# Rows 0 and 1: rotary keys copied out of PSUM by ScalarE and turned on GpSimd, with a new instruction order

## The reference

```python
_, idx = jax.lax.top_k(I, kk)                  # 96 keys for each query
key_c = (c_kv @ W_uk)[bi, idx]
kr_sel = (x @ W_kr)[bi, idx]                   # picked rotary keys
angles_k = jnp.arange(kk)[:, None] * theta[None, :] + delta    # by rank in the list
key_r = _pope(kr_sel, angles_k[None, None, :, :])
scores = (einsum(q_c, k_c) + einsum(q_r, key_r)) * scale
```

## Time and profile before

| | |
|---|---|
| median of 3 runs | 1168.19 us (1167.93 to 1173.78) |
| profiled execution, its own time | 1168.04 us |
| its span | 1166.3 us |
| busy: PE, DVE, ACT, POOL | 822.1, 890.1, 599.5, 299.4 us |
| granted TensorE clock, mean | 0.841 of full |

### The profile page before, as it was taken

The page is one execution under the profiler, slowest core; times in us unless marked ns, Lnnn a source line. Parts: engine busy times, 40 slices in busy tenths (PEclk is TensorE's granted clock), DMA queues, the critical chain, the costliest instruction groups (busy, mean ns, idle before and its releaser), DMA issues.

```text
span 1166.3 us, 29414 instructions
## 1 busy us (share of the span) xinstructions
PE 822.1 (70%) x11808; PEld 509.2 (44%) x11808; DVE 890.1 (76%) x2076; ACT 599.5 (51%) x1311; POOL 299.4 (26%) x224
## 2 busy tenths in 40 slices
PE   5666868888758885587674877467677774667784
...
DMA packets 85079, 72.20 MB, mean 62 GB/s; under 512 B 24784, under 2 KB 63696, under 8 KB 84752
## 3 DMA queue, kind: packets, MB, share of 16 engines
...
## 4 chain that ended last, share of the span: by engine, by line
DVE 30%; PE 24%; issue 18%; ACT 13%; POOL 8%; DMA 4%; SPq 2%; DVEq 0%; POOLq 0%; ACTq 0%
POOL big L1512 4%; PE bank L660 4%; DVE Y L2045 3%; DVE bank L1955 3%; PE bank L882 3%; PE bank L847 2%; ACT relu_s L1178 2%; DVE onehot L1735 2%; DVE relu_s L1623 2%; DMA big<-comb_rows 1%; DVE SG L1955 1%; POOL XP L1519 1%; SPq L593 1%; ACT QBD L1217 1%; PE bank L1006 1%
## 5 line engine op out<-in xcount | busy, mean ns | idle before, releaser
L1512 POOL TENSOR_TENSOR big<-DU,BC 128x1024 f32<-128x1024 f32 x64 | 150.5, 2358 | 168.0 <-DVE DU L1938 121.8
L1396 ACT ACTIVATE bank<-DEL,Aneg 128x512 f32<-128x512 f32 x128 | 87.8, 690 | 118.3 <-DVE CV L1962 42.1
L847 PE MATMUL bank<-onehot,tparts 128*32 128x256 bf16 x3840 | 124.8, 283 | 25.0 <-DVE onehot L1735 17.9
L847 PEld LDWEIGHTS bank<-onehot,tparts 128*32 128x32 bf16 x3840 | 101.1, 100 | 52.6 <-issue 30.6
L1006 PE MATMUL bank<-XP,CO 128*128 128x512 f32 x128 | 77.1, 720 | 31.2 <-POOL XP L1519 25.4
L1955 DVE TENSOR_TENSOR_SCAN bank<-bank,big 128x512 f32<-128x512 f32 x72 | 87.7, 1218 | 7.7 <-POOL big L1512 7.3
L1006 PE MATMUL bank<-CV,CO 128*128 128x512 f32 x128 | 74.8, 696 | 25.9 <-POOL CV L1519 23.0
L1451 POOL TENSOR_TENSOR fac<-em,den 128x16 f32<-128x16 f32 x16 | 5.0, 315 | 311.5 <-DVE den L1603 311.5
L1735 DVE TENSOR_SCALAR onehot<-ib,CO 128x1024 bf16<-128x1024 f16 x160 | 80.7, 548 | 2.6 <-PE bank L847 1.8
L1178 ACT ACTIVATE relu_s<-bank,nml 128x192 f32<-128x192 f32 (+1 forms) x128 | 52.8, 425 | 44.2 <-DVE nml L1691 43.9
L882 PE MATMUL bank<-GT,QBD 128*32 128x32 f32 x3072 | 54.5, 201 | 23.5 <-issue 15.3
...
## 6 DMA issues: line engine op xcount, KB each, us to landing
BC<-bc_rows SPq DMA_DIRECT2D x128, 256.0 KB, 4.4
...
rows_bounce<-RO SPq DMA_DIRECT2D x256, 8.5 KB
...
```

The lines of the kernel that those rows point to most:

```text
L847: m = mm(own.bank[3 - c % 2][32 * bb:32 * bb + 32, 256 * kind:256 * kind + 256], own.tparts[:, kt, part, 32 * kind:32 * kind + 32], onehot ...
L1396: A(own.bank[STATE_BANKS[j]][:, :], own.DEL[:, j, :], ACT.Exp, scale=Aneg[:, j, n:n + 1]).then_inc(dA_ok.sem, dA_ok.up(b))
L1512: pool.tensor_tensor(own.dBu[:, n % 2, :, :], own.DU[:, :, :], own.BC[:, n % ROWS_AHEAD, 0:1, :].to_broadcast([P, 2, L]), ALU.mult).then_i ...
```

## The change

For rows 0 and 1 (`turned_by_gpsimd`), DVE's multiplication L1744 goes: 32 instructions, four for each of eight tiles. In its place ACT copies the rotary half of the bank to SBUF (alternately into `SRd` and `PR`, which are free at that time) ahead of its latent copy, and POOL multiplies that copy by `rank_turn` into `GT[:, 1:3]`, with a new signal `gk_ok`. PE waits for `gk_ok` of all four chunks ahead of the picked scores; ACT waits for it ahead of chunks 2 and 3, whose copies go into a buffer used before. Some signals are merged to make room for the new one (the counting signals `hold_*` share one semaphore; gates and routing share signals), with the same waits. Rows 2 and 3 are as before. `ORDER` is new for all five engines over the whole program.

```diff
+        def turned_by_gpsimd(b):
+
+            return b < 2
...
                     pe.wait_ge(gt_ok.sem, gt_ok.at(b, 4 * i + 4))
+                    if turned_by_gpsimd(b):
+                        pe.wait_ge(gk_ok.sem, gk_ok.at(b, 4 * i + 4))
                     pe.wait_ge(g_sb.sem, g_sb.at(b, 4 * i + 4))
...
+                        if turned_by_gpsimd(b):
+                            if c >= 2:
+                                act.wait_ge(gk_ok.sem, gk_ok.at(b, 4 * i + c - 1))
+                            elif i >= 1:
+                                act.wait_ge(psum_ok.sem, psum_ok.at(b, i))
+                            A((own.SRd, own.PR)[c % 2][:, :, :].rearrange("p x j -> p (x j)"), own.bank[3 - c % 2][:, 256:512], ACT.Copy)
                         A(GT[:, 0, 8 * c:8 * c + 8, :].rearrange("p t j -> p (t j)"), own.bank[3 - c % 2][:, 0:256], ACT.Copy).then_inc(g_sb.sem, g_sb.up(b))
...
+                    if turned_by_gpsimd(b):
+                        for c in range(4):
+                            yield PART
+                            pool.wait_ge(g_sb.sem, g_sb.at(b, 4 * i + c + 1))
+                            PT(GT[:, 1:3, 8 * c:8 * c + 8, :], (own.SRd, own.PR)[c % 2][:, :, :].unsqueeze(1).to_broadcast([P, 2, 8, 32]),
+                               rank_turn[:, :, :].unsqueeze(2).to_broadcast([P, 2, 8, 32]), ALU.mult).then_inc(gk_ok.sem, gk_ok.up(b))
...
-                        TT(GT[:, 1:3, 8 * c:8 * c + 8, :], picked[:, 1:2, :, :].to_broadcast([P, 2, 8, 32]),
-                           rank_turn[:, :, :].unsqueeze(2).to_broadcast([P, 2, 8, 32]), ALU.mult)
+                        if not turned_by_gpsimd(b):
+                            TT(GT[:, 1:3, 8 * c:8 * c + 8, :], picked[:, 1:2, :, :].to_broadcast([P, 2, 8, 32]),
+                               rank_turn[:, :, :].unsqueeze(2).to_broadcast([P, 2, 8, 32]), ALU.mult)
                         dve.transpose(own.G[:, 8 * c:8 * c + 8, :], picked[:, 0, :, :]).then_inc(gt_ok.sem, gt_ok.up(b))
...
 ORDER = {
     "sync": (
-        7, 7, 11, 11, 16, 16, 16, 16, 16, 16, 32, 6, 1, 3, 15, 25, 16, 7, 5, 1, 11, 10, 1, 17, 36, 4, 11, 25,
+        0, 7, 18, 11, 16, 16, 16, 16, 16, 16, 32, 9, 2, 1, 3, 5, 1, 19, 26, 7, 11, 1, 5, 11, 1, 16, 31, 4, 5,
```

More of the change, by code:

```diff
@@ L330, in build @@
         s_setp = semaphore("setup_tensor")
-        hold_dve, hold_pe = semaphore("hold_vector"), semaphore("hold_tensor")
+        hold_dve = hold_pe = semaphore("hold_vector_or_tensor")
         hold_pool = hold_sp = semaphore("hold_gpsimd_or_sync")
@@ L365, in build @@
         gt_ok = signal("picked_keys_ready")
+        gk_ok = signal("picked_keys_turned_by_gpsimd")
         sr_ps = signal("picked_scores_in_psum")
@@ L400, in build @@
         rl_ps = signal("router_logits_in_psum")
-        rl_e = signal("router_exp_ready")
+        rl_e = signal("routing_exp_ready")
         comb_ok = signal("comb_ready")
-        ct_ps = signal("comb_t_in_psum")
-        ct_sb = signal("comb_t_in_sbuf")
+        ct_ps = signal("comb_then_gates_t_in_psum")
+        ct_sb = signal("comb_then_gates_t_in_sbuf")
         ga_ps = signal("gate_in_psum")
@@ L438, in build @@
         pm_ok = signal("gate_shifted")
-        pe_ok = signal("gate_exp_ready")
         mk_ok = signal("choice_ready")
@@ L443, in build @@
         cum_ok = signal("slots_taken_by_rows_ready")
-        gT_ps = signal("gates_t_in_psum")
-        gT_sb = signal("gates_t_in_sbuf")
         bias_ps = signal("bias_in_psum")
@@ L1054, in rest @@
                     m = turn(own.bank[2][0:NE2, i * P:(i + 1) * P], own.gate[:, i, :])
-                m.then_inc(gT_ps.sem, gT_ps.up(b))
+                m.then_inc(ct_ps.sem, ct_ps.up(b))
                 yield
-                pe.wait_ge(gT_sb.sem, gT_sb.at(b, 1))
+                pe.wait_ge(ct_sb.sem, ct_sb.at(b, 2))
                 pe.sem_inc(hold_pe, 1)
@@ L1408, in rest @@
                 act.wait_ge(pm_ok.sem, pm_ok.at(b, 1))
-                A(own.pr[:, 1, :, :], own.pr[:, 0, :, :], ACT.Exp).then_inc(pe_ok.sem, pe_ok.up(b))
+                A(own.pr[:, 1, :, :], own.pr[:, 0, :, :], ACT.Exp).then_inc(rl_e.sem, rl_e.up(b))
                 yield
                 yield
-                act.wait_ge(gT_ps.sem, gT_ps.at(b, 1))
-                A(own.GTs[:, :], own.bank[2][0:NE2, :], ACT.Copy).then_inc(gT_sb.sem, gT_sb.up(b))
+                act.wait_ge(ct_ps.sem, ct_ps.at(b, 2))
+                A(own.GTs[:, :], own.bank[2][0:NE2, :], ACT.Copy).then_inc(ct_sb.sem, ct_sb.up(b))
                 yield
@@ L1989, in rest @@
                 yield
-                dve.wait_ge(pe_ok.sem, pe_ok.at(b, 1))
+                dve.wait_ge(rl_e.sem, rl_e.at(b, 2))
                 dve.tensor_reduce(own.ps1[:, 1, :], own.pr[:, 1, :, :], AX.X, ALU.add).then_inc(vec.sem, vec.up(b))
@@ L2134 @@
     "sync": (
-        7, 7, 11, 11, 16, 16, 16, 16, 16, 16, 32, 6, 1, 3, 15, 25, 16, 7, 5, 1, 11, 10, 1, 17, 36, 4, 11, 25,
-        16, 7, 5, 1, 11, 11, 1, 16, 33, 29, 9, 1, 1, 6, 4, 1, 1, 1, 2, 2, 1, 1, 17, 23, 2, 2),
+        0, 7, 18, 11, 16, 16, 16, 16, 16, 16, 32, 9, 2, 1, 3, 5, 1, 19, 26, 7, 11, 1, 5, 11, 1, 16, 31, 4, 5,
+        1, 2, 19, 9, 5, 16, 7, 16, 7, 1, 2, 2, 1, 3, 1, 3, 17, 25, 29, 17, 1, 1, 1, 1, 2, 6, 3, 10, 28, 2, 2),
     "tensor": (
[10 rows of a table removed]
-    "scalar": (
[12 rows of a table removed]
[9 rows of a table added]
+    "scalar": (
[12 rows of a table added]
     "gpsimd": (
-        1, 1, 20, 20, 15, 15, 15, 15, 21, 15, 8, 7, 32, 12, 15, 20, 1, 3, 20, 22, 2, 1, 6, 20, 32, 12, 15, 20,
-        1, 3, 14, 38, 17, 5, 18, 28, 11, 1, 3, 2, 1, 2, 1, 1, 3, 2, 2, 2, 1, 1, 1, 2, 1, 1, 1, 1, 2, 2, 1, 2,
-        14, 23),
+        0, 1, 7, 6, 18, 18, 1, 1, 18, 18, 2, 1, 17, 3, 1, 15, 4, 1, 28, 25, 32, 28, 15, 3, 21, 30, 7, 1, 1,
+        16, 32, 12, 3, 2, 12, 15, 15, 21, 2, 3, 5, 20, 14, 5, 14, 8, 1, 2, 3, 1, 2, 2, 2, 15, 17, 1, 2, 1, 2,
+        3, 13, 37),
     "vector": (
[11 rows of a table removed]
[11 rows of a table added]
 }
```

## The result

The changed kernel takes 1191.01 us (median of 4 runs, 1182.32 to 1192.98) against 1168.06 us for the kernel before on the same chip (4 runs, 1165.50 to 1173.78): ratio 1.0177, interval 1.0131 to 1.0223. The ratios in this document are those on record, which compare only runs within 1.5% of the fastest of their kernel; they aren't quotients of the medians and differ from these by up to 0.4 points (the quotient here is 1.0196). The forecast was 1161.1 with a range up to 1175, so it missed in sign. The profiled execution took 1190.45 us, its span 1188.7.

What follows compares the result with a forecast made beforehand. From 60 to 330 us no engine is full, so freeing DVE alone can't shorten it one for one. 1168.0 - 1.9 (first stretch) + 0 (middle) - 5 (end) = 1161.1 us; range 1150 to 1175.

Steps and rivals of the forecast that it cites:

- What bounds the kernel: Attention of rows 0 and 1, 60 to 330 us: no engine full, DVE no more loaded than PE, GpSimd has room.
- Removed: First stretch: 32 DVE multiplications go, 21.9 us of DVE, of which 4.0 us lie on the chain: -4.0.
- ACT: Rows 0 and 1: 32 added copies of 0.37 us, 11.9 us of ACT, hidden inside a tile; waits cost nothing.
- POOL's own time: Rows 0 and 1: 32 multiplications at 1.28 us each, 41 us of POOL, bounded by 1.27 and 1.46.
- Last chunk: End of each tile: PE's scores wait for POOL, +0.5 us a tile; +2.0 for four cases, +4 for all eight.
- POOL against DVE: First stretch: POOL's work slows DVE by 0.11 us a microsecond, some 5 us for 41 us of POOL.
- 16 one-hots at +0.144 make +2.3: First stretch's chain: each of 16 one-hots slowed by 0.144 us beside POOL's work, +2.3 us.
- the forecast's band of 0.50 to 0.60: Before 345 us: expected mean one-hot time in us if the forecast holds; over 0.8 would show the third rival.
- The third rival: First stretch: POOL's turn and the next one-hot meet each time; +13.4, with the end's -5 1176.4 us; chance 0.18.
- Half of the costs covered by the new order: First stretch: other row's work hides half of 4.3 us of costs, giving -1.9 instead of +0.3.
- Middle, 0 within 4: Later attention, 345 to 850 us: no changed instructions, only another interleaving; 0, with 4 us either way.
- End, -5: Program's end: four groups of row 2's sums go ahead of row 3's last scan step; -5, bounds 0 and -7.4.

Runs made afterwards that it cites:

- e4: The kernel before plus ScalarE's 32 copies of the rotary half that nobody reads; ratio 1.0011 over the kernel before.
- c2: e2 plus ScalarE's 32 idle copies of the rotary half; ratio 1.0076 over the kernel before.
- e2: Old code (VectorE multiplies, no GpSimd turns) in the changed kernel's new order; ratio 1.0035 over the kernel before.
- f1: f0 plus the idle GpSimd multiplications of d1; 1176.59 us, ratio 1.0037 over the kernel before.
- f0: d4 again in more rounds; 1166.79 us against 1172.13 for the kernel before, ratio 0.9944.
- d1: e2 plus 32 idle GpSimd multiplications, started by each latent copy, that only a later DMA waits for; ratio 1.0183 over the kernel before.
- e6: Changed kernel with the old order up to a point in row 1's last tile, new order behind; ratio 1.0045 over the kernel before.
- d4: Old code (VectorE multiplies) with the orders of e6; ratio 0.9956 over the kernel before.
- b0: The kernel before, unchanged, run again on another chip for a profile; 1175.9 us beside a median of 1172.77.
- d2: d1 with each tile's four idle multiplications started together behind its last transpose; ratio 1.0184 over the kernel before.

## Why the prediction was wrong

**What bounds the kernel** was read right (no engine full), and the wrong thing was drawn from it: room on GpSimd is not free where GpSimd's work stops VectorE.

**Removed** (-4.0) and **ACT** (nothing): 32 multiplications went, as said, and ScalarE's copies cost 0.1 (e4) to 0.4 points (c2, against e2), not to be told from nothing; the forecast for ACT stands. That the 32 multiplications gave 4.0 us back on the chain is not borne out: idle work that frees nothing costs no more than the turns that free 21.9 us of VectorE (0.87 beside 0.95 points, 1.49 beside 1.35 to 1.42).

**POOL's own time**: 1.28 forecast, 1.32 measured. Right.

**Last chunk** (+2.0, 4 to 8 waits charged to GpSimd): one wait of 2.2 us was charged to it, and those for the transpose fell from 4.3 to 3.4. Together 5.6 instead of 4.3: right in size, and small.

**POOL against DVE** is the step that failed, "By that rate 41 us of POOL cost DVE some 5 us", and with it the term "16 one-hots at +0.144 make +2.3". VectorE was held 24.0 us, 0.57 a microsecond of turn and not 0.11, and GpSimd's load alone, idle, cost 10 to 17 us of the program's time (f1 against f0, d1 against e2). The rate came from three groups in a stretch where 155 us of GpSimd work lay beside all kinds of VectorE work, and the sum then charged one-hots alone. But here GpSimd doesn't start at random: the latent copy that starts the turn also starts VectorE's transpose, and what stands behind the transpose meets the turn. With the multiplication gone, nothing covers it, as I read it: idle work beside VectorE's multiplication holds VectorE 11.4 us (f1 against f0, one-hots 560 ns), the turn in its place 23.8 (e6 against d4, one-hots 12.0 of it). The mean of the one-hots, 564, fell into the forecast's band of 0.50 to 0.60, which I had taken for its confirmation; over two thirds of the held time lay on other instructions. The mean was a bad witness: of the 84 one-hots up to 366 us eight took 1.15 us or more, in b0 none.

The chain from 60 to 330 us, here in the changed kernel and below it in e2, shows how much of this became time:

```profile
by line: issue 19.3%; PE bank L849 10.2%; PE bank L662 6.1%; PE bank L886 6.0%; DVE onehot L1751 5.2%; DVE relu_s L1639 4.1%; ACT QBD L1221 4.0%; DVE top L1669 2.3%; PE bank L745 2.2%; DVE score L1674 1.9%; DVE ml L1702 1.9%; ACT PBD L1255 
...
by line: issue 18.7%; PE bank L849 8.4%; PE bank L886 6.3%; PE bank L662 5.7%; DVE onehot L1753 3.8%; ACT QBD L1221 3.4%; ACT PBD L1255 3.0%; DVE ml L1704 2.7%; DVE score L1658 2.7%; DVE G L1765 2.6%; DVE top L1671 2.4%; PE bank L745 2.3%; 
```

One-hots have 14.0 us of it and not 7.8, 10.3 in e2; `relu_s` L1639 has 11.1, where neither L1623 before nor its counterpart in e2 is among the rows shown. The share called issue, time in which the engine waited for nothing that the profile shows, went from 14.5% to 19.3%, 13 us more, and nearly all of that is in e2 too, where GpSimd turns nothing: it came with the new order. Why holds of this sum cost some 16 us in the new start and 4 to 11 in the old one stays open.

**The third rival** had the mechanism and a chance of 0.18. Its price, +13.4 for the first stretch, is near the 11 to 17 us that the turns cost (0.95 to 1.42 points); but that is in part luck: it charged all 32 turns, and eight one-hots were held for about a turn, with one-hots 6.2 us longer on the chain and not 13.4. Its sign of over 0.8 us for the mean one-hot was wrong for the same reason. Its place was too narrow as well: d2 shows that the load costs as much when one-hots don't meet it. "A mean of 0.144 also with POOL beside them" was the argument against it, and it was an average over places.

**Half of the costs covered by the new order** (-1.9 for the stretch) failed in sign. The new start costs 0.85 points by itself (e2 against d4 and f0), some 10 us. In e2's trace one-hots wait 7.0 us for TensorE's picks (9.9 and 4.9 in the two profiles of the changed kernel), which they didn't in the old order (0.2). That the moved positions of the one-hots are the cause is only argued: no run exchanges VectorE's list alone.

**Middle, 0 within 4**: it moved -5.4 and +13.6. The forecast said itself that over 4 us would make it wrong. All kernels of the table with the new rest show the second (276 to 283 us beside row 3's attention instead of 268), whatever their code, and the first against b0's 288.2 (279 to 283). It is the order; which part of it is open.

**End, -5** (bounds 0 and -7.4): -6.4 in the changed kernel, -5.2 to -6.6 in the others of the table with the new rest. Right, with its working: 41.9 us from the last scan step where under 45 was said.

The sum, corrected: +17.8 where -1.9 stood, 2.8 ahead of it that belongs to no step, +8.2 where 0 stood, -6.4 where -5 stood: +22.4.
